# Five fused stages: other places for the start-up work, the overlap of neighbouring stages and the matmuls that hold the clock

## The reference

```python
h = tokenizer(x)                        # depthwise convolution of 5 taps, stride 2 -> 188 tokens; norm over a row's
                                        # whole tokens and channels; yn > 0 ? yn : alpha * yn
h = h + alibi_attention(layernorm(h))   # 8 heads of 32, causal softmax(q k / sqrt(32) + slope * (s - t)), out @ Wo + bo
h = h + expert_attention(layernorm(h))  # 4 heads of 16 with 4 query experts each; causal softmax, a gate over the
                                        # experts, layernorm, a small MLP, layernorm, a gate over the heads
h = h + polynomial_attention(layernorm(h))  # 8 heads of 8: 0.5 (qn.kn)^2 + s^2 (qn.kn) + s^4, not causal,
                                        # through sums of kn_i kn_j v over all tokens; divided by the norm column
h = h + mixture(layernorm(h))           # 8 experts: y_e = gelu(xn @ W1[e] + b1[e]) @ W2[e] + b2[e], top 2 by
                                        # logits xn @ Wr + br, weighted by a softmax over the two
```

## Time and profile before

| | us |
|---|---|
| median of 3 runs | 1454.28 |
| lowest and highest | 1453.88, 1455.33 |
| the profiled execution | 1455.6 |
| its span | 1453.9 |
| mean granted clock of TensorE | 0.952 |
| TensorE busy | 1320.3 (91%) |
| VectorE busy | 1051.4 (72%) |
| ScalarE busy | 809.2 (56%) |
| GpSimd busy | 738.7 (51%) |

### The profile page before, as it was taken

One profiled execution on the slowest core, in us unless ns is written; L12 is line 12 of the kernel. 1 busy time (PEld: TensorE's weight loads), 2 busy tenths in 40 slices (PEclk: granted clock), 3 DMA queues, 4 the chain that ended last, 5 costly groups with the idle time before them and its releaser, 6 DMA issues.

```text
span 1453.9 us, 46760 instructions
## 1 busy us (share of the span) xinstructions
PE 1320.3 (91%) x15948; PEld 952.1 (65%) x16045; DVE 1051.4 (72%) x3413; ACT 809.2 (56%) x2178; POOL 738.7 (51%) x1502
## 2 busy tenths in 40 slices
PE   1699999999799999999999999954899999999997
PEld 1355555555456666666666666633799888999996
DVE  8366666667447788888888888875577774488886
ACT  4365555555356666666666666623445542566663
POOL 7565555554325555555555555554454453454440
PEclk9999999999899999999999999975799996899998
DMA  3000000000000000000000000000000000000000
GB/s 151 1 2 1 0 0 0 0 0 0 2 1 2 2 2 0 0 0 0 0 0 0 0 0 0 0 1 1 1 1 0 0 0 1 2 6 10 6 10 13
DMA packets 6982, 7.93 MB, mean 5 GB/s; under 512 B 6273, under 2 KB 6273, under 8 KB 6785
## 3 DMA queue, kind: packets, MB, share of 16 engines
q1 hardware_dynamic: 6912, 7.02, 1.4%
HBM read 5.48 MB, written 1.54 MB: 5 GB/s over the span
## 4 chain that ended last, share of the span: by engine, by line
PE 76%; DVE 9%; issue 4%; ACT 4%; POOL 2%; DVEq 0%; ACTq 0%; POOLq 0%
PE bank_one L1363 12%; PE bank_five L904 6%; PE bank_five L1472 4%; PE bank_quad L1453 4%; PE bank_quad L1427 4%; PE bank_quad L883 3%; PE bank_pair L1943 3%; PE bank_pair L937 3%; PE bank_pair L2249 3%; PE bank_pair L1417 2%; PE bank_five L1964 2%; PE bank_five L1895 2%; PE bank_five L1476 2%; PE bank_quad L2239 2%; PE bank_pair L1412 2%
## 5 line engine op out<-in xcount | busy, mean ns | idle before, releaser
L1346 POOL TENSOR_SCALAR_AFFINE_SELECT ex_pT<-ex_pT 128x512 f32<-128x512 f32 (+1 forms) x256 | 127.2, 520 | 185.0 <-ACT ex_pT L1580 178.6
L2324 ACT ACTIVATE mo_hT<-bank_quad,mo_b 128x188 f32<-128x188 f32 x256 | 86.1, 418 | 68.4 <-PE bank_quad L2239 68.2
L1643 DVE TENSOR_REDUCE ex_negmaxA<-bank_pair 128x4 bf16<-128x512 f32 x128 | 88.6, 692 | 36.1 <-PE bank_pair L1413 33.9
L1882 POOL TENSOR_TENSOR ta_kk<-ta_ext 94x320 f32<-94x320 f32 x64 | 60.0, 955 | 105.5 <-DVE ta_qkn L2086 105.5
L1560 ACT ACTIVATE ex_pT<-bank_quad 128x496 f32<-128x496 f32 x128 | 74.8, 584 | 66.7 <-PE bank_quad L1456 65.7
L1030 ACT ACTIVATE al_pT<-bank_quad 128x496 f32<-128x496 f32 x128 | 75.1, 587 | 49.5 <-PE bank_quad L887 49.3
L1336 POOL TENSOR_TENSOR ex_zrstd<-ex_zvar,neg_half 94x16 f32<-94x16 f32 x34 | 100.6, 2958 | 2.8
L2249 PE MATMUL bank_pair<-wsb,mo_hT 128*94 128x64 f32 x1024 | 96.0, 247 | 4.1 <-DVE mo_weighted L2388 3.3
L2249 PEld LDWEIGHTS bank_pair<-wsb,mo_hT 128*94 128x94 f32 x1024 | 90.2, 163 | 6.6 <-DVE mo_weighted L2388 4.0
L1134 DVE RECIPROCAL al_rec<-bank_five 128x188 f32<-128x188 f32 x64 | 84.7, 1323 | 2.8 <-PE bank_five L904 2.8
L816 POOL TENSOR_SCALAR_AFFINE_SELECT al_pT<-al_pT 128x512 f32<-128x512 f32 (+1 forms) x128 | 63.5, 519 | 45.7 <-ACT al_pT L1030 27.9
(11 more groups left out here) (364 smaller groups left out, 3991.2 us busy)
## 6 DMA issues: line engine op xcount, KB each, us to landing
tok_xin<-x_t SPq DMA_DIRECT2D x4, 760.0 KB, 6.5
wsb<-weights SPq DMA_DIRECT2D x1, 2308.0 KB, 13.4
out<-stream SPq DMA_DIRECT2D x16, 94.0 KB
tok_par<-tok_w SPq DMA_DIRECT2D x1, 4.5 KB, 1.8
```

The source lines that it names most:

```text
L1346: nc.gpsimd.affine_select(out=view, in_=view, compare_op=ALU.is_ge, fill=0.0, base=shift, pattern=[[0, NH], [1, cols]], channel_multiplier ...
L1643: red(negmaxA[e % 2][:, D::32], R[:, 0, :].rearrange("p (n s) -> p n s", n=NH), AX.X, ALU.max, negate=True)\
L2324: nc.scalar.activation(hT[p][:, e, :], HB[e // 2 % 2][:, (e % 2) * N:(e % 2 + 1) * N], ACT.Gelu, bias=b1[:, e:e + 1]).then_inc(h_ready, 1)
```

## The change

1. **Tokenizer, GpSimd.** The masked biases move behind the masks of the expert stage. Zeros, masks and fills move one chunk later each: zeros behind the first chunk, masks behind the second, fills behind the third. The last chunk's join, transposes and stores are done in two halves.
2. **Bias folding.** The nine matmuls and the two adds move into the tokenizer: TensorE's behind its first `turn`, VectorE's behind the third `join`, with a bank of their own.
3. **Weight parts.** The low part moves to ALiBi's turn 4 and the last one to its turn 33; the gate biases move from turn 4 to 5.
4. **ALiBi to expert.** The list becomes `[0, 0, 1, 0, 1]`, so ALiBi's last turn stands ahead of the expert stage's turn 1. The 16 fillers ahead of its first unit become two behind each of five steps of turn 1 and six ahead of the unit.
5. **Expert to polynomial.** The list becomes `[0, 1, 1, 1, 1, 1, 1]`. GpSimd runs the polynomial turn in two parts inside of the expert turn: the norms ahead of the expert's power, the products `kk` at its end. TensorE's waits for the expert stage move into turn 1.
6. **Polynomial to mixture.** `full(t)` no longer ends with turn 35: five fillers more in turn 36 and one each in the next two. The mixture begins without the folding and its waits.

The diff, cut to its core:

```diff
-            expert_zeros()
+            masked_biases()
...
             for c in range(CHUNKS):
                 powers(c)
                 negative_side(c)
                 if c == 0:
+                    expert_zeros()
+                if c == 1:
                     taylor_masks()
-                if c == 1:
+                if c == 2:
                     taylor_fills()
...
             def turn(c):
-                pe.wait_ge(out_ready, c + 1)
                 for k in range(BANKS):
+                    pe.wait_ge(out_ready, c + 1 + (k if c == CHUNKS - 1 else 0))
...
+                if c == 1:
+                    fold()
...
+            if isinstance(t, int) and t == 4:
+                weight_parts_low()
+            if isinstance(t, int) and t == 5:
                 gate_biases()
-            if isinstance(t, int) and t == 5:
                 taylor_temperatures()
+            if isinstance(t, int) and t == B + 1:
+                weight_parts_last()
...
-    return Stage(sem, [0, 0, 1, 1, 0], gpsimd, tensor, scalar, vector)
+    return Stage(sem, [0, 0, 1, 0, 1], gpsimd, tensor, scalar, vector)
...
-            if isinstance(u, int) and u == 0:
-                pe.wait_ge(*alibi_done["early_outputs"])
             if isinstance(u, int) and u in WARM_AT:
-                keep_busy(WARM)
-            keep_busy(FILLERS)
+                keep_busy(6 if u == 0 else WARM)
...
+                if e == 2 and beside:
+                    beside(0)
...
-            if isinstance(t, int) and t == B + 1:
-                weight_parts_low()
-            if isinstance(t, int) and t == B + 2:
-                weight_parts_last()
-
-        return Turns(body)
+            if beside:
+                beside(1)
+
+        return Turns(body, within=True)
...
-    return Stage(sem, [0, 0, 1, 2, 2, 1, 1], gpsimd, tensor, scalar, vector)
+    return Stage(sem, [0, 1, 1, 1, 1, 1, 1], gpsimd, tensor, scalar, vector)
...
         def full(t):
 
-            return valid(t - 7) and not (isinstance(t, int) and t >= B + 4)
+            return valid(t - 7)
...
-        pe.wait_ge(*taylor_done["XT"])
-        for e in range(E):
-            nc.tensor.matmul(FOLD[:, e:e + 1], w("w1", C)[:, e * HID:(e + 1) * HID], w("beta_t", C), start=True, stop=True)
-        nc.tensor.matmul(FOLD[0:P, E:2 * E], w("beta_t", C).broadcast_to([C, P]), w("wr", C), start=True, stop=True)\
-            .then_inc(fold_full, 1)
         return Turns(body)
```

118 lines of the change are left out of this document (74 added, 44 removed).

## The result

The changed kernel takes 1429.23 us in the median of four runs (1427.47 to 1430.59), the kernel before 1454.12; the ratio is 0.9835, 95% interval 0.9813 to 0.9856. The forecast was 1427 in 1418 to 1441. The profiled execution of the changed kernel has a span of 1428.8 us against 1453.9, so 25.1 us less. It is the slowest of the four executions (1430.59 us, mean granted clock 0.962; the two fastest have 0.964), so a stretch of its trace can be some us longer than in the others.

What follows compares the result with a forecast made beforehand. TensorE bounds steady stretches; its clock halves at three stage boundaries, where VectorE and GpSimd waits also count. Terms 1.8 + 0.6 − 0.8 − 9.5 − 20 = −27.9 us from 1455.6, median 1.3 lower: 1426.4, stated 1427, range 1418 to 1441.

Steps and rivals of the forecast that it cites:

- part 5: Polynomial stage's drain into the mixture: folding gone and full clock instead of half, taken −20 us, bounds −22 and −0.4.
- Part 1: Tokenizer: later fills delay the fourth power, halves give some back, folding costs 0; taken +1.8 us, bounds 0 and +2.5.
- step on the fills: Tokenizer: GpSimd's 2.8 us of fills, less 0.65 us of waiting, make the fourth power 2.1 us later, up to 2.5.
- Part 2: Weight parts moved into ALiBi: turn 4 +0.5 us, gate biases +0.1, turn 33 0; together +0.6, bounds 0 and +1.8.
- Part 3: ALiBi to expert: projections in front and fillers in the chain's waits; taken −0.8 us, bounds −2.2 and +4.
- Part 4: Expert's drain into the polynomial stage: contention gone and one polynomial turn per drain turn; −9.5 us, bounds −13 and −5.
- the contention: Expert's drain: two VectorE instructions beside GpSimd's weight parts lose 2.9 and about 1.9 us; both go.
- rival C: Expert's drain: only the contention goes, turn 6 or GpSimd's order eats the rest; 1431 to 1436 us; chance 0.07.
- The folding's step: Mixture's start: the bias folding and its waits go, −3.2 us, removing TensorE's only hole before the clock's fall.
- the wait of 1.9 us: Mixture's first transposes wait about 1.9 us for GpSimd's chain of splits, which half the clock used to hide.
- rival A: Polynomial to mixture: clock falls at the 1.9 us wait, about half the gain left, −10 us, so 1436.5; chance 0.2.
- My own sign of being wrong: Polynomial stage's end into the mixture: the forecast is wrong if granted clock 0.50 stands there for over 15 us.

Runs made afterwards that it cites:

- e12: The kernel before with only the bias folding moved to the tokenizer; 1441.2 us, ratio 0.9931.
- e1: The changed kernel with fillers in the polynomial stage's drain, two at the end of turn 34 and five at the end of turn 35; 1426.1 us, ratio 0.9822.
- e2: The changed kernel without the seven fillers in turns 36 to 38; 1428.9 us, ratio 0.9859.
- e9: The changed kernel with the sixteen fillers in one block ahead of the expert stage's first unit; 1434.0 us, ratio 0.9875.
- e10: The changed kernel with ALiBi's last turn behind the expert stage's turn 1 again, fillers still scattered; 1428.1 us, ratio 0.9840.
- e5: The kernel before with only the weight parts moved into ALiBi; 1451.0 us, ratio 0.9983.
- e4: The changed kernel with the old list of the expert stage, up to two polynomial turns per drain turn; 1427.8 us, ratio 0.9847.
- e6: The changed kernel with GpSimd's polynomial turn whole and behind the expert's turn again; 1434.0 us, ratio 0.9869.
- e11: e7 without the seven end fillers in turns 36 to 38; 1421.5 us, ratio 0.9799.
- e7: e1 with GpSimd's order in the tokenizer as in the kernel before, folding and halves kept; 1422.3 us, ratio 0.9784.

## Why the prediction was right

The time was within 2.2 us of the forecast, but that is partly luck: the mechanism failed in part 5, and the errors of the terms cancelled.

Part 1, the tokenizer: +1.8 forecast, +1.3 at ALiBi's start. The step on the fills held (power 1.9 us later, 2.1 forecast), and the halves gave 0.65, just under the 0.7 to 1.5 forecast. Failed: that the nine folding matmuls cost nothing there; alone they delay ALiBi by 0.8 us (e12). In the changed kernel that isn't seen: its third power comes no later than before (39.57 and 39.72), and the fills set the fourth. What I hadn't seen is that TensorE's first matmuls of ALiBi run at half clock and that the clock came back at about the same moment in both traces: its first transposes took 0.52 us at 60.75 before and 0.33 at 61.23 after. (The granted clock shows it only in the changed kernel, 0.50 from 58 to 60; before, it is given as 1.00, and the lengths speak against that.) By the first weighing in the steady order only 0.2 us of the 1.3 were left. That is luck too. In e1 and e2 that repayment didn't come (24.1 and 24.4 us from the start to that weighing, 23.2 in the changed kernel).

Part 2, weight parts: +0.6 forecast; from +0.2 at 79.93 the lag grows to 0.4 and then 0.65 by turn 5, so +0.45. Turn 33 cost 0 as said. VectorE's instructions beside GpSimd's subtraction kept their 1.32 and 0.35 us. This agrees with the second half of the rule in the Trainium skill ("SBUF — State Buffer", "Who interferes with whom"), that a VectorE instruction with at most one input in SBUF is left alone by GpSimd.

Part 3: −0.8 forecast, −1.8 measured. The chain's start was forecast at 391.8, came at 392.9; the first score (L1443) at 399.9 to 401.1, came at 400.8. Counted from the last weighing the first score is 0.3 later than before (forecast 0 to 1.1) and what follows 2.1 nearer (2.2). The 0.8 us set down for fillers that stand where the chain is ready were not spent: that term was mis-sized. What carries the part is the scattering of the fillers (4.8 us, e9), and then the projections in front add about 1 us (e10, one trace), which without it lose 3.0.

Part 4: −9.5 forecast, −10.6 measured, and the beats came within 1 us of those forecast (960.6, 974.5, 985.5, 995.2, 1006.0 against 961.7, 975.9, 986.6, 997.3, 1008.0 less 1.1 for the earlier start). Of its two steps the contention held (4.8 forecast, 5.0 in e5), though its first 2.9 us were read from one instruction and lie in two (e5). The other, that one polynomial turn in each drain turn is what shortens them, failed: e4 has two and loses 0.3, e6 keeps one and loses 5.1. The turns were long for GpSimd's order; I had counted that order as a part of rival C, as a price.

Part 5: −20 forecast, −14.0 measured. The folding's step was right (3.2 us and the clock, e12), and so was the sum for a clock that stays up: with the holes filled the stretch is 20.0 us shorter than before (32.06 against 52.04, e1). Failed: that the clock would hold at the wait of 1.9 us ahead of the mixture's first transposes. The wait was 0.98 us, and behind it and the 0.54 us ahead of it the clock fell all the same, for 13 us. This is the place and the wait of rival A (0.2), which gave −10. My own sign of being wrong, 0.50 for over 15 us, was set too wide for it; the other, the transposes some 25 us after the end of the steady stage, came at 31.8 (1193.09 to 1224.84). And the end fillers, which I took for the means, cost 1.0 us where that can be read (e11 against e7) and give nothing that a trace shows (e2, e12).

The other errors hid it: 1.6 and 0.15 us too much cost in parts 1 and 2, 1.0 and 1.1 too little gain in parts 3 and 4, against 6.0 too much gain in part 5 and 0.6 in stretches forecast at 0.

## What to carry to other kernels

Where TensorE is the bound and its clock is down for long, look at the last microseconds ahead of the fall: a hole of one to three microseconds there (nine tiny matmuls behind a wait; a transposes' input that GpSimd finishes 1 us late) cost 12 us here in one place and 3 to 6 in the other. Filling it with matmuls that stay inside the wait cost nothing. Where the chain runs over VectorE and GpSimd, the same fillers raised the clock and not the speed: what the clock gave, fillers ahead of ready work took. There look for the instruction that stands ahead of another on an engine without need. And before crediting a schedule with a gain, undo its parts one at a time: here the list of turns, which looked like the change, was worth 0.3 us of 10.6. An equal end doesn't show that a part did nothing: the halves' 0.65 us were hidden by the folding's 0.7.
